# Filing stage of a graph layer on one core: the word product and the low half of the normed x made by GpSimd instead of VectorE

## The reference, cut to what matters

```python
xn = layernorm(x)
x = x + gnn(xn, edges) + mix(xn)      # two graph convolutions, linear attention
x = x + ffn(layernorm(x))             # 8 experts, the best 2 of them for a node

def graph_conv(x, edges, W0, b0, W1, b1):
    src = concatenate([edges[:, 0], edges[:, 1]])
    dst = concatenate([edges[:, 1], edges[:, 0]])
    deg = maximum(segment_sum(ones, dst), 1)
    agg = segment_sum(x[src], dst) / deg[:, None]
    return x @ W0 + b0 + agg @ W1 + b1
```

## Time and profile before

| | us |
|---|---|
| median of 3 runs | 2392.94 (2387.78 to 2393.01) |
| the profiled execution, its own time | 2393.36 |
| its span, first to last instruction | 2391.8 |
| VectorE's rounds, first L1062 to last L1062 | 38.4 to 404.9 |

### The profile page before, as it was taken

How to read it: one execution, slowest core, us unless ns; L and a number is a source line. 1 busy time by engine, 2 the same in 40 slices (tenths; PEclk the granted TensorE clock), 3 DMA queues, 4 the chain that set the end, 5 groups by cost and what they waited for, 6 DMA issues and landing times.

```text
span 2391.8 us, 53412 instructions
## 1 busy us (share of the span) xinstructions
PE 2131.0 (89%) x15340; PEld 1322.6 (55%) x15341; DVE 1611.5 (67%) x4907; ACT 1204.1 (50%) x2432; POOL 352.3 (15%) x427
## 2 busy tenths in 40 slices
PE   2545557999999999999799999999999998699997
PEld 2434445555555555555355554444444443599996
DVE  6999998799999999999444342454444445355554
ACT  2445455455555555555455553444444444466664
POOL 1000000000000000000111110112112112266655
PEclk9665566899999999999899999999999999899998
DMA  3111112622222222222212124555555554655552
GB/s 81 40 34 36 38 32 70 181 110 118 110 117 110 116 114 115 113 117 110 96 51 101 50 70 176 186 207 188 191 204 186 195 200 164 165 95 92 90 92 46
DMA packets 132542, 275.62 MB, mean 115 GB/s; under 512 B 30478, under 2 KB 85951, under 8 KB 130291
## 3 DMA queue, kind: packets, MB, share of 16 engines
q1 hardware_dynamic: 103411, 221.23, 26.5%
q0 software_dynamic: 25216, 44.98, 8.6%
q10 hardware_dynamic: 3840, 8.52, 1.1%
HBM read 137.14 MB, written 132.95 MB: 113 GB/s over the span
## 4 chain that ended last, share of the span: by engine, by line
PE 80%; DVE 8%; issue 4%; DVEq 4%; ACT 1%; POOL 1%; DMA 1%; ACTq 1%; SPq 0%; POOLq 0%
PE bank L2127 44%; PE bank L2118 6%; PE bank L2348 6%; PE bank L2333 6%; PE bank L2280 5%; PE bank L2268 5%; DVE big L1034 2%; PE bank L2283 2%; DVE big L1048 1%; DVEq L1063 1%; PE bank L2315 1%; DVEq L1031 1%; DVEq L1044 1%; PE bank L2135 1%; PE bank L1996 1%
## 5 line engine op out<-in xcount | busy, mean ns | idle before, releaser
L2127 PE MATMUL bank<-RW,big 128*128 128x512 f16 (+1 forms) x4900 | 1180.1, 380 | 4.9 <-DMA big<-a_dram 4.7
L2127 PEld LDWEIGHTS bank<-RW,big 128*128 128x128 f16 x4900 | 443.8, 98 | 401.6 <-issue 9.1
L1784 ACT ACTIVATE big<-bank 128x512 f16<-128x512 f32 (+1 forms) x640 | 371.7, 581 | 317.5 <-PE bank L2118 317.5
L1181 DVE TENSOR_TENSOR big<-iotaB,keys 128x512 f16<-128x512 f16 x1300 | 451.7, 416 | 7.9 <-issue 7.8
L2118 PEld LDWEIGHTS bank<-big 128*128 128x128 f16 x2560 | 190.8, 98 | 111.5 <-issue 1.2
L2118 PE MATMUL bank<-big 128*128 128x128 f16 x2560 | 247.2, 219 | 0.7 <-issue 0.7
L899 POOL DMA_INDIRECT out_dram<-big x112 | 178.4, 1593 | 136.2 <-ACT big L1941 102.3
L842 POOL DMA_DIRECT2D big<-in_L_ffn_W_dram x8 | 6.4, 804 | 1145.0 <-DVE R L1240 1142.1
L1932 ACT ACTIVATE big<-bank,b1A,iscA 128x256 f32<-128x256 f32 x224 | 114.3, 560 | 99.2 <-PE bank L2333 93.9
L2333 PE MATMUL bank<-big,RW 128*128 128x256 f16 x1344 | 157.9, 275 | 3.7 <-ACT big L1921 3.7
L2348 PE MATMUL bank<-RW,big 128*128 (+1 forms) x1344 | 155.9, 273 | 0.0
(11 more groups left out here) (396 smaller groups left out, 2971.5 us busy)
## 6 DMA issues: line engine op xcount, KB each, us to landing
big<-a_dram SPq DMA_DIRECT2D x49, 832.0 KB, 6.0
big<-a_dram SPq DMA_DIRECT2D x49, 768.0 KB, 4.5
a_dram<-big SPq DMA_DIRECT2D x49, 640.0 KB, 3.0
a_dram<-big SPq DMA_DIRECT2D x49, 512.0 KB, 2.6
a_dram<-big SPq DMA_DIRECT2D x49, 448.0 KB, 2.5
big<-rows_dram SPq DMA_DIRECT2D x56, 265.0 KB
big<-in_x_dram SPq DMA_DIRECT2D x96, 128.0 KB, 2.1
big<-in_L_ffn_W_dram POOLq DMA_DIRECT2D x16, 512.0 KB, 4.6
```

The source lines that it names most:

```text
L1181: last = v.tensor_tensor(out[q].rearrange("p b (m k) -> p b m k", k=2), inturn(iotaB[:, :], QB, P // 2), twice(kd[:, q * QB:(q + 1) * QB, ...
L1784: a.activation(Ab[q][:, 0:n], banks[BB(q)][:, 0:n], ACT.Copy).then_inc(s_ab, 1)
L2127: last = mm(bank[:, :], blk(q, c), src, start=(u == 0), stop=(u == T))
```

## The change

GpSimd gets a loop of 49 rounds behind its constants. Each has `values(t)`, the product that was L1034, and `low(t)`, which does in two instructions (scale, then subtract) with a drain between them what L1069 did in one. VectorE's `onehots` and its rounds lose both. VectorE's one-hot of tile t now waits also for `s_val`, since GpSimd reads the buffer that it overwrites; SP's clearing of a region after the stage waits for `s_val` too.

```diff
--- before.py
+++ after.py
@@ -596,6 +596,7 @@
             sp.wait_ge(s_const, 2)
             sp.wait_ge(s_xl, T)
+            sp.wait_ge(s_val, T)
             blank(0, at_pairs // D)
             sp.wait_ge(s_flag, 2)
             blank(at_pairs // D, T - 6)
@@ -769,6 +770,28 @@
                                     pattern=[[-P, 2], [D // HEADS, HEADS], [0, D // HEADS]],
                                     channel_multiplier=-1).then_inc(s_const, 1)
             nc.gpsimd.memset(pwait[:, :], 0.0)
+
+            def values(t):
+
+                pool.wait_ge(s_oh, t + 1)
+                if t >= 3:
+                    pool.wait_ge(s_filed, t - 2)
+                nc.gpsimd.tensor_tensor(V[t % 3].bitcast(F32).rearrange("p (c u) -> p c u", c=CAP),
+                                        OH[t % 2].rearrange("p (c u) -> p c u", c=CAP),
+                                        endsF[:, t * CAP:(t + 1) * CAP].rearrange("p (c o) -> p c o", o=1)
+                                        .to_broadcast([P, CAP, U]), ALU.mult).then_inc(s_val, 1)
+
+            def low(t):
+                pool.wait_ge(s_xlo, t + 1)
+                pool.wait_ge(s_xhi, t + 1)
+                nc.gpsimd.tensor_scalar(xlo, xs[:, 0:D], S, None, ALU.mult)
+                pool.drain()
+                nc.gpsimd.tensor_tensor(xlo, xlo, R2[:, bass.ds(t * 2 * D, D)], ALU.subtract).then_inc(s_xl, 1)
+
+            for t in range(T):
+                values(t)
+                low(t)
+
             pool.wait_ge(s_flag, 2)
             def wait(s, n):
@@ -1026,14 +1049,10 @@
                 oh = OH[par].rearrange("p (c m k) -> p c m k", c=CAP, k=2)
                 if t >= 2:
                     dve.wait_ge(s_before, t - 1)
+                    dve.wait_ge(s_val, t - 1)
                 v.tensor_tensor(oh, inturn(iotaU[:, :], CAP, U // 2), twice(key2[:, sl, :], CAP, U // 2),
                                 ALU.is_equal).then_inc(s_oh, 1)
                 dve.drain()
-                if t >= 3:
-                    dve.wait_ge(s_filed, t - 2)
-                v.tensor_tensor(V[t % 3].bitcast(F32).rearrange("p (c u) -> p c u", c=CAP),
-                                OH[par].rearrange("p (c u) -> p c u", c=CAP), deep(endsF[:, sl], [P, CAP, U]),
-                                ALU.mult).then_inc(s_val, 1)
             def ranks(t, par):
@@ -1062,12 +1081,6 @@
                 v.reciprocal(rstd[:, :], sums[:, 3:4])
                 dve.drain()
                 v.tensor_tensor(offs[:, :], sums[:, 1:2], rstd[:, :], ALU.mult).then_inc(s_stat, 1)
-
-            def low(t):
-                dve.wait_ge(s_xhi, t + 1)
-                dve.wait_ge(s_xlo, t + 1)
-                v.scalar_tensor_tensor(out=xlo, in0=xs[:, 0:D], scalar=S, in1=R2[:, bass.ds(t * 2 * D, D)],
-                                       op0=ALU.mult, op1=ALU.subtract).then_inc(s_xl, 1)
             def scales1():
                 dve.wait_ge(s_sr, 1)
@@ -1115,7 +1128,6 @@
                 if t + 1 < T:
                     onehots(t + 1, (t + 1) % 2)
                 ranks(t, t % 2)
-                low(t)
                 if t % PACK == PACK // 2 and t // PACK + 1 < NG:
                     prepare(t // PACK + 1)
                 if t == 12:
```

## The result

The changed kernel takes 2419.78 us (median of 4 runs, 2417.07 to 2420.62), the kernel before beside it 2390.41 (2387.78 to 2393.01): a ratio of 1.0122, 95% interval 1.0109 to 1.0135. It is slower by 29 us. The forecast had the sign and, with 2411 to 2502, a range that holds the time, but its likeliest time was 2471, 78 over the profiled execution of before: the size was more than twice too large.

A forecast was written before the change was run, and what follows sets the result against it. VectorE's list was taken to bound the filing rounds. 1.74 us more in each of 42 plain rounds (73) plus 5 for the six with `prepare` made 78: 2393.36 + 78 = 2471 us, range 2411 to 2502.

The forecast's parts named there:

- What bounds the stage: Filing rounds: VectorE's own list sets the 6.20 us round, and a microsecond there is one of the whole time.
- What else would hold the round: Reciprocal waiting for ScalarE's deviation: a round is 5.45 us at best, not 4.74, so 0.75 won in a plain round.
- Whether the two engines can run together: Filing rounds: reading GpSimd instructions and VectorE's two-tensor instructions exclude each other from both sides; this decides the sign.
- What GpSimd has to do: GpSimd's product, scale and subtraction per round: 2.30, 0.38 and 0.66, taken as 3.34 us, between 2.03 and 3.87.
- The sum: Plain round, one-hot to one-hot: 4.44 + 3.34 + 0.16 = 7.94 us, 1.74 more than 6.20.
- That all of it comes one after the other behind R1: End of each round: scale, subtraction, the offset's single value, then the next tile's product, all before the next one-hot; round 7.94.
- The rounds with `prepare`: Six rounds: GpSimd's work can lie under one-tensor instructions; between nothing and 1.74 us each, half taken, 5 us.
- The forecast's 73 + 5: Loss over the stage: 73 us in 42 plain rounds and 5 in the six with `prepare`, sum 78.
- Its signs: Profile after: rounds take 444 us, GpSimd's product 2.3 or longer, L1053 or its successor some 2 longer, reduction 0.69, TensorE's clock lower.
- A sharing at +45: Rival on the shared port: GpSimd fills gaps, round 7.2 us, +45, so 2438; chance 0.20.
- That VectorE is never held up: Rival at the one-hot L1053: only GpSimd waits, the round is ScalarE's 5.45, -41, so 2352; chance 0.12.

The follow-up runs named there:

- the fills: The changed kernel with memsets in place of GpSimd's arithmetic; only the stage is readable: first to last reciprocal 324.9 us, 41.7 less than the kernel before.

## Why the prediction was right in sign and wrong in size

**What bounds the stage**: right. VectorE's list set the round, and a microsecond of the stage was about one of the whole time (26.2 in the stage, 23.7 in the execution).

**What else would hold the round**: right in the total. 41 us to be won was worked out; 41.7 and 47.0 were measured with nothing to read on GpSimd. That it fits so well is in part luck. The forecast had 0.75 from each plain round and 1.46 from each with `prepare`. With the fills a plain round gave 0.92 (6.41 to 5.49 in the mean, and many take 5.07, less than the 5.45 that ScalarE was to need) and one with `prepare` only 0.5 (16.2 to 15.7).

**Whether the two engines can run together**: right, and now shown from both sides. The rule of the Trainium skill (SBUF — State Buffer, "Who interferes with whom") holds as to who contends: the offset's 1.58 us agrees. As to how long, the section says of a first one in VectorE's 2-port modes that it gets the shared pair "for the whole instruction", and the forecast took that for two inputs as well. If it is read as the length of the record, the numbers differ: with a record of 2.71 VectorE was let in after 0.87. The measurement decides.

**What GpSimd has to do**: this step failed, "I take 3.34, a little under the case of two inputs in turn". The sum put 3.34 us of kept port into each round. Where the GpSimd instruction starts on a free port, VectorE was let in after 1.71 for the product (2.30 predicted), 0.25 for the scale (0.38) and 0.52 for the subtraction (0.66; L789 starts at 197.01, and the offset, which needs 0.16, ends at 197.69), 2.5 in all. In most rounds of the change the product and the subtraction had been waiting for VectorE, and then it is 1.57 and about 0.39, with the scale 2.2 in all. With 2.2 in the place of 3.34 the forecast's own sum gives 4.44 + 2.2 + 0.16 = 6.8, 0.6 more than before, and the median plain round is 6.77. That two inputs are read in turn was right; the 1.15 ns a value was not. It came from records of `affine_select`, and what counted was 0.86 ns a value read, or 0.79 where the instruction had been waiting.

**That all of it comes one after the other behind R1**: not so in detail. The product was met by L1061 behind the one-hot, or by the offset, as in the rows; the scale lay mostly under the reduction; and ahead of 18 of the 49 reciprocals VectorE waited for ScalarE, which the sum did not have. These go both ways, and the sum with 2.2 does not say how much each is worth.

**The rounds with `prepare`**: 5 us taken, 11.4 measured, and the reason given for taking so little, that GpSimd's work can lie under its one-tensor instructions, does not hold. They are kept out as well. Their third one, 0.23 us before, in one of the six rounds:

```profile
237.36 1.85 POOL L779 TENSOR_TENSOR big<-big,R 128x1000 f32<-128x1000 f16 x1
237.41 1.89 DVE L1003 TENSOR_SCALAR R<-R 128x140 int32<-128x140 int32 x1
```

and the first one over all six rounds, also 0.23 before:

```profile
L1002 DVE TENSOR_SCALAR R<-R 128x140 int32<-128x140 int32 x6 | 7.2, 1198 | 0.0
```

Part of this is only moved. The product that would have met the next round has run here, so the six rounds right behind take 5.4 us instead of 6.3, 5 less in all; that is why the 42 plain rounds have lost 14.8 and not 42 x 0.56. The forecast's 73 + 5 is thus 14.8 + 11.4 as measured. The 17.7 us that it gave to a round with `prepare` before the change was misread too: it took all plain rounds at 6.20, but two of them take 9.7 and 8.9, and the six take 16.2. No term of the sum used it.

**Its signs.** The reduction kept its 0.69 and L1061 grew by 1.48, as said. The rounds were to take 444 us and took 393, and TensorE's granted clock, which was to fall, was 0.64 in both kernels.

**The rivals.** A sharing at +45 had a better size than the forecast, for the wrong reason: the port is kept one after the other, only for less time. That VectorE is never held up did not happen.

## What to carry to other kernels

In this kernel, work moved from VectorE to GpSimd was paid for in VectorE's time wherever GpSimd read while VectorE had an instruction on two tensors: count the values that GpSimd reads, both tensors of it, at the measured 0.86 ns each, against VectorE's own duration for the same work, and not the length of GpSimd's record. Then look for VectorE instructions that are not hurt (here a reduction that takes 0.77 us of VectorE's list) and give GpSimd just what fits under them, with a semaphore that starts it there: 8 columns so placed won 15 us where all 20, started at once, lost 30. Before anything is moved, see what the round comes to with that work made by nobody.

## What the runs showed of the hardware that was not expected

A GpSimd instruction with one tensor in can have a much longer record than one with two (2.71 against 1.85 us for 1000 values, a `tensor_scalar` from 16 to 32 bits against a product) and yet keep VectorE out for half as long.

VectorE's `tensor_scalar` from SBUF to SBUF on integers waits even for a GpSimd fill, which reads nothing, while the instructions on two tensors did not. In the run with fills:

```profile
202.10 0.94 POOL L779 MEMSET big<- 128x1000 f32 x1
202.85 0.27 DVE L1001 TENSOR_SCALAR R<-R 128x140 int32<-128x140 int32 x1
...
203.14 1.04 DVE L1003 TENSOR_SCALAR R<-R 128x140 int32<-128x140 int32 x1
203.16 0.93 POOL L781 MEMSET big<- 128x1000 f32 x1
204.10 0.16 DVE L1004 TENSOR_SCALAR R<-R 128x140 int32<-128x140 int32 x1
```

L1003 needs 0.23 when GpSimd is idle and ends, at 204.18, 0.09 after the fill. In the change the casts of `prepare` are held up as well, L1008 by up to 1.7 us. So "one tensor" is not enough to be safe from GpSimd: the reduction and the reciprocal were, this one was not.
